# Attention queries: rotary rows crossed by four DMAs instead of two matrix products, and attended values in two portions in half of the pairs

## What is computed

```python
q = rms_norm(hidden_states @ wq_a, q_a_norm_w) @ wq_b      # rank 64, then 16 heads of 64 + 64
q_nope, q_pe = (q[..., :QK_NOPE], q[..., QK_NOPE:])
...
def rotate_half(x):
    x1, x2 = jnp.split(x, 2, axis=-1)
    return jnp.concatenate([-x2, x1], axis=-1)

def apply_rope(x, cos, sin):
    b, h, s, d = x.shape
    x = x.reshape(b, h, s, d // 2, 2).transpose(0, 1, 2, 4, 3).reshape(b, h, s, d)
    return x * cos + rotate_half(x) * sin
...
attn = jnp.einsum('bhqd,bhkd->bhqk', query_states, key_states) * SOFTMAX_SCALE
attn = jax.nn.softmax(attn.astype(jnp.float32), axis=-1)
out = jnp.einsum('bhqk,bhkd->bhqd', attn, value_states)
```

## Time and profile before

| | us |
|---|---|
| three runs, median (lowest to highest) | 1085.58 (1083.63 to 1086.48) |
| the profiled execution | 1089.22 |
| its span | 1087.4 |
| busy in the span: PE, DVE, ACT, POOL | 1014.7, 739.5, 518.5, 477.3 |

### The profile page before, as it was taken

One profiled execution on the slowest core, in us unless ns is written; L12 is line 12 of the kernel. 1 busy time (PEld: TensorE's weight loads), 2 busy tenths in 40 slices (PEclk: granted clock), 3 DMA queues, 4 the chain that ended last, 5 costly groups with the idle time before them and its releaser, 6 DMA issues.

```text
span 1087.4 us, 22864 instructions
## 1 busy us (share of the span) xinstructions
PE 1014.7 (93%) x6183; PEld 802.6 (74%) x6184; DVE 739.5 (68%) x1677; ACT 518.5 (48%) x1133; POOL 477.3 (44%) x418
## 2 busy tenths in 40 slices
PE   5459999999889999999999999999999889999995
PEld 4438888887557777777778777777688558888884
DVE  7446666745577788877887788888556746766642
ACT  2033334422366677767776677777401214443421
POOL 3733444433343744646464644443125514443422
PEclk9989999999899999999999999999999999999998
DMA  9646454422101123222232313232576434545230
GB/s 332 171 156 152 106 112 112 105 49 30 59 1 49 41 78 99 79 69 73 76 99 79 85 54 98 80 98 79 178 235 216 177 112 112 159 109 112 47 57 8
DMA packets 88899, 112.57 MB, mean 104 GB/s; under 512 B 10257, under 2 KB 65809, under 8 KB 88785
## 3 DMA queue, kind: packets, MB, share of 16 engines
q1 hardware_dynamic: 73936, 94.20, 28.6%
q0 software_dynamic: 14304, 16.87, 9.0%
q10 hardware_dynamic: 576, 0.53, 0.2%
HBM read 64.14 MB, written 51.34 MB: 106 GB/s over the span
## 4 chain that ended last, share of the span: by engine, by line
PE 84%; DVE 8%; issue 3%; ACT 1%; DMA 1%; another core or an unknown queue 1%; POOL 1%; POOLq 0%; DVEq 0%; SPq 0%; ACTq 0%
PE bank L1766 11%; PE bank L1793 11%; PE bank L1583 7%; PE bank L1581 7%; PE bank L1585 7%; PE bank L1754 5%; PE bank L1756 5%; PE bank L1755 5%; PE bank L1593 4%; PE bank L1595 3%; PE bank L1594 3%; PE bank L1566 3%; PE bank L1866 3%; PE bank L1741 2%; PE bank L1742 2%
## 5 line engine op out<-in xcount | busy, mean ns | idle before, releaser
L929 ACT ACTIVATE shared<-bank,small 128x512 f32<-128x512 f32 x256 | 176.7, 690 | 90.8 <-DVE small L1394 89.8
L1394 DVE TENSOR_REDUCE small<-bank 128x1 f32<-128x512 f32 x256 | 174.9, 686 | 41.8 <-PE bank L1756 41.7
L846 ACT CAST split_rows_and_inner<-bank 128x512 fp32r<-128x512 f32 x78 | 45.8, 587 | 238.3 <-PE bank L1566 177.7
L1766 PE MATMUL bank<-constants,shared 128*128 128x128 f32 x1024 | 156.3, 275 | 2.3 <-ACT shared L929 0.7
L1766 PEld LDWEIGHTS bank<-constants,shared 128*128 128x128 f32 x1024 | 122.2, 141 | 45.0 <-issue 13.9
L1583 PE MATMUL bank<-expert_weights_low,split_rows_and_inner 128*128 x312 | 144.2, 462 | 0.0
L1585 PE MATMUL bank<-expert_weights_high,split_rows_and_inner 128*128 x312 | 143.1, 459 | 0.0
L1581 PE MATMUL bank<-expert_weights_high,split_rows_and_inner 128*128 x312 | 125.1, 401 | 2.7 <-DVE split_rows_and_inner L1173 2.5
L1754 PE MATMUL bank<-expert_weights_high,shared_split 128*128 128x512 f32 x256 | 122.7, 479 | 2.4 <-POOL shared_split L672 1.4
L663 POOL TENSOR_TENSOR shared<-shared 128x512 f32<-128x512 f32 x32 | 41.3, 1289 | 189.0 <-DVE shared L1404 185.5
L1178 DVE TENSOR_TENSOR split_rows_and_inner<-bank,split_rows_and_inner 128x512 fp32r<-128x512 f32 x78 | 53.9, 692 | 100.9 <-ACT split_rows_and_inner L846 98.9
(11 more groups left out here) (201 smaller groups left out, 2194.5 us busy)
## 6 DMA issues: line engine op xcount, KB each, us to landing
rows_by_expert<-empty_rows SPq DMA_DIRECT2D x34, 516.0 KB, 5.3
expert_weights<-w SPq DMA_DIRECT2D x32, 512.0 KB
shared<-rows_by_expert SPq DMA_DIRECT2D x78, 129.0 KB
expert_weights<-wo SPq DMA_DIRECT2D x16, 512.0 KB
shared<-inverse_sums SPq DMA_DIRECT2D x64, 128.0 KB, 2.9
attended_transposed<-shared SPq DMA_DIRECT2D x32, 256.0 KB, 5.1
expert_weights<-attended_transposed SPq DMA_DIRECT2D x2, 2048.0 KB, 10.8
shared<-attended_transposed SPq DMA_DIRECT2D x2, 2048.0 KB
```

The costliest lines, as they stand in the source:

```text
L929: nc.scalar.activation(prob[k % 4], bank[k % 4][:, :], ACT.Exp, bias=negmax[:, k % 8:k % 8 + 1], accum_out=psum[par][:, hh * GT + qt:hh * ...
L1394: V.tensor_reduce(negmax[:, k % 8:k % 8 + 1], bank[k % 4][:, :], AX.X, ALU.max, negate=True).then_inc(max_ready, 1)
L1766: last = tr(bank[4 + k % 2][:, c * P:(c + 1) * P], prob[k % 4][:, c * P:(c + 1) * P], ident)
```

## The change

1. The products of part 1 are left out for pairs 2 to 31. In their place ACT copies part 0 from bank 7 to SBUF (`queries_unturned`, at k = 4, in pair 0 at k = 5, behind the preparation's copy and ahead of the exponential). SP moves it with four DMAs of 32 partitions each, which cross the halves, into the buffer ropeB (`turn_queries`), and DVE multiplies that by sine. The sign is in the table of sines now. The second rope product of DVE goes from k = 7 to k = 0 of the next pair. DVE's first rope product waits for ACT's copy of the same bank.
2. On SP `spread` is cut into `inverse_out` and `inverse_back`, and the four DMAs with their waits stand between them.
3. POOL makes the high and low part of two of three weights from pair 2 on; four one-time DVE instructions that write the turned weights write two pairs' and not eight pairs' worth.
4. In pairs p > 0 with remainder 0, 3, 4 or 7 by eight and in the last eight (`apart`), the attended values are made in two portions of 16 matmuls, one at k = 1 and one at k = 4 behind the scores. There `take_output` moves from k = 2 to k = 6, and DVE's copy of tile 4 stands behind the row maximum and not ahead of it. Waits for the buffers of tiles 0 to 3 now look at the first portion (`o_half`).

```diff
     c[:, C_COS:C_SIN] = np.tile(cos.T, (4, 1))
-    c[:, C_SIN:C_ALL] = np.tile(sin.T, (4, 1))
+    c[:, C_SIN:C_ALL] = np.concatenate([-sin.T, sin.T, -sin.T, sin.T])
     ids = (np.arange(NT)[None, :] * P + np.arange(P)[:, None]).astype(np.int32)
...
             return bank[(7, 6, 3)[part]] if among(p, 0) else bank[7]
+
+        def apart(p):
+
+            return p > 0 and (p // PAIRS + 1 == B or p % PAIRS in (0, 3, 4, 7))
...
-            def spread(p, par):
+            def turn_queries(p):
+
+                sp.wait_ge(unturned_sb, p - 1)
+                sp.wait_ge(rope_ready, p)
+                for a in range(4):
+                    b = a + 1 - 2 * (a % 2)
+                    sp.dma_start(ropeB[a * HALF:(a + 1) * HALF], unturned[b * HALF:(b + 1) * HALF]).then_inc(turned_in, 16)
+
+            def inverse_out(p):
                 sp.wait_ge(invT_sb, p + 1)
                 sp.dma_start(invd[p:p + 1, :].rearrange("a (k q) -> (a k) q", k=8), invT).then_inc(inv_stored, 16)
+
+            def inverse_back(p, par):
                 sp.wait_ge(inv_stored, (p + 1) * 16)
...
                 load_prep(g)
-            spread(0, 0)
-            spread(1, 1)
+            for p in range(2):
+                turn_queries(p + 2)
+                if p == 1:
+                    inverse_back(0, 0)
+                inverse_out(p)
+            turn_queries(4)
+            inverse_back(1, 1)
             load_prep(3)
                 store(p, p % 2)
-                spread(p + 2, p % 2)
+                inverse_out(p + 2)
+                if p + 5 < NPAIR:
+                    turn_queries(p + 5)
+                inverse_back(p + 2, p % 2)
                 empty_rows(p)
...
                 store(p, p % 2)
-                spread(p + 2, p % 2)
+                inverse_out(p + 2)
+                inverse_back(p + 2, p % 2)
             sp.wait_ge(o_psum, NPAIR)
...
-                src = wpair[:, p % PAIRS, :, :]
+                parts_ = slice(0, 3) if among(p, 0, 1) else slice(0, 3, 2)
+                src = wpair[:, p % PAIRS, parts_, :]
                 if p > 1:
                     pool.wait_ge(qz_psum, p - 1)
-                nc.gpsimd.tensor_copy(wch[par], src).then_inc(wc_high, 1)
+                nc.gpsimd.tensor_copy(wch[par][:, parts_, :], src).then_inc(wc_high, 1)
                 pool.wait_ge(wc_high, p + 1)
                 pool.sem_inc(pool_issue, 1)
-                nc.gpsimd.tensor_tensor(wcl[par], src, wch[par].bitcast(F32), ALU.subtract).then_inc(wcur_ready, 1)
+                nc.gpsimd.tensor_tensor(wcl[par][:, parts_, :], src, wch[par][:, parts_, :].bitcast(F32),
+                                        ALU.subtract).then_inc(wcur_ready, 1)
...
                 if k == 2 and not among(p, 0):
-                    act.wait_ge(o_psum, p)
+                    act.wait_ge(o_half, p)
                 nc.scalar.copy(pT[:, pT_place(par, k), :, :],
...
                 nc.scalar.copy(qh[par][hh][rows_], query_bank(p, 2)[rows_, :]).then_inc(qz_high, 1)
+
+            def queries_unturned(p):
+                act.wait_ge(qa_psum, p + 1)
+                if not among(p, 2):
+                    act.wait_ge(turned_in, (p - 2) * 64)
+                nc.scalar.copy(unturned, bank[7][:, :]).then_inc(unturned_sb, 1)
...
                             high_keys(b, 2, 6)
+                    if k == (5 if first else 4) and p + 2 < NPAIR:
+                        queries_unturned(p + 2)
                     if not (last and k > 5):
...
                                     norm_w[:, 0:1], None, ALU.mult)
-                    last = V.tensor_scalar(wpair[:, :, 1, at + (1 - two) * HALF:at + (2 - two) * HALF], src[:, :, hh, :],
-                                           norm_w[:, 0:1], -1.0 if two else 1.0, ALU.mult, ALU.mult)
+                    last = V.tensor_scalar(wpair[:, 0:2, 1, at + (1 - two) * HALF:at + (2 - two) * HALF], src[:, 0:2, hh, :],
+                                           norm_w[:, 0:1], None, ALU.mult)
             last.then_inc(wa_ready, 1)
...
                         dve.wait_ge(rope_ready, p)
+                    if not among(p, 0, 1):
+                        dve.wait_ge(unturned_sb, p - 1)
                     V.tensor_tensor(ropeA, query_bank(p, 0)[:, :], qcos, ALU.mult).then_inc(ropeA_sb, 1)
                 else:
-                    dve.wait_ge(qb_psum, p + 1)
-                    V.tensor_tensor(ropeB, query_bank(p, 1)[:, :], qsin, ALU.mult).then_inc(ropeB_sb, 1)
+                    if among(p, 0, 1):
+                        dve.wait_ge(qb_psum, p + 1)
+                        turned = query_bank(p, 1)[:, :]
+                    else:
+                        dve.wait_ge(turned_in, (p - 1) * 64)
+                        turned = ropeB
+                    V.tensor_tensor(ropeB, turned, qsin, ALU.mult).then_inc(ropeB_sb, 1)
...
                 if k == 0 and not among(p, 0, 1):
-                    dve.wait_ge(o_psum, p - 1)
+                    dve.wait_ge(o_half, p - 1)
                 if k == 4 and not among(p, 0):
...
                         ropes(1, k - 1)
+                    if k == (6 if apart(p) else 2) and not first:
+                        take_output(p - 1, 1 - par)
                     if k == 2 and not first:
-                        take_output(p - 1, 1 - par)
                         invert_sums(p - 1, 1 - par)
                         ropes(p + 2, 0)
-                    if k == 7 and not among(p, NPAIR - 2, NPAIR - 1):
-                        ropes(p + 2, 1)
-                    if k in BY_DVE:
+                    if k == 0 and not first and not last:
+                        ropes(p + 1, 1)
+                    late_copy = k == 4 and apart(p)
+                    if k in BY_DVE and not late_copy:
                         copy_pT(p, par, k)
...
                         row_max(p * 8 + k + AHEAD, k + AHEAD)
+                    if late_copy:
+                        copy_pT(p, par, k)
                     if p // PAIRS + 1 < B:
...
                         pe.wait_ge(invT_sb, p - 2)
+                elif among(p, 1):
+                    pe.wait_ge((ropeA_sb, ropeB_sb)[part - 1], p + 1)
                 elif not among(p, 0):
-                    pe.wait_ge((ropeA_sb, ropeB_sb)[part - 1], p + 1)
+                    pe.wait_ge(ropeA_sb, p + 1)
                 to = query_bank(p, part)
...
-            def attend(p, par):
-
-                pe.wait_ge(v_kept, p // PAIRS + 1)
-                pe.wait_ge(raw_sb, p)
-                bank_back(p // PAIRS + 1, p % PAIRS, 1)
+            def attend(p, par, halves):
+
+                if 0 in halves:
+                    pe.wait_ge(v_kept, p // PAIRS + 1)
+                    pe.wait_ge(raw_sb, p)
+                    bank_back(p // PAIRS + 1, p % PAIRS, 1)
                 wait_pT(pe, p, BY_ACT[-1])
                 wait_pT(pe, p, BY_DVE[-1])
-                for half in range(2):
+                for half in halves:
                     for c in range(GT):
...
                                       values[:, p // PAIRS, c, :], pT[:, a:b + 1:b - a, c, :], start=(c == 0), stop=(c == GT - 1))
-                last.then_inc(o_psum, 1)
+                    last.then_inc((o_half, o_psum)[half], 1)
...
                     if k == 1 and not first:
-                        attend(p - 1, 1 - par)
+                        attend(p - 1, 1 - par, (0,) if apart(p) else (0, 1))
+                    if k == 4 and apart(p):
+                        attend(p - 1, 1 - par, (1,))
                     if k == 2 and not first:
...
                         queries(p + 2, par, 0)
-                    if k == 3 and b < B:
+                    if k == 3 and b < B and not apart(p) and not first:
                         pe.wait_ge(raw_sb, p)
...
                             turn_keys(b, 2, 6)
-                    if k == 6 and p + 2 < NPAIR:
-                        queries(p + 2, par, 1)
                     if k == 6 and j in (1, 2, 5):
...
             inverse_transpose(NPAIR - 1, 1)
-            attend(NPAIR - 1, 1)
+            attend(NPAIR - 1, 1, (0, 1))
```

4 lines of the change are left out of this document (added).

## The result

| | before | after |
|---|---|---|
| median, us (lowest to highest, runs) | 1086.2 (1080.45 to 1089.63, 20) | 1089.7 (1086.09 to 1093.63, 20) |
| ratio of the times, with its 95% interval | | 1.0036 [1.0023, 1.0049] |
| span of the profiled execution | 1087.4 | 1090.7 |
| from the first attended values to the last, us | 457.97 | 462.14 |

The change makes the kernel slower by 3.9 us (2.5 to 5.3): small, but outside zero. I had forecast 1085.4 us, no difference. The last line of the table counts from the first start of an attended group to the last, and takes in the 31 pairs; there the loss is 4.17 us, so it lies in the attention. What lies outside took 629.4 us before and 628.6 after.

What follows compares the result with a forecast made beforehand. PE's program was taken as the bound (84% of the span). Terms -8.3 + 2.9 - 3.0 + 8.2 summed to -0.2 us, so 1085.4 us from a median of 1085.58; range 1074 to 1093.

Steps and rivals of the forecast that it cites:

- The laden pairs, +8.2: 12 pairs with whole attended values: DVE waits for ACT's copy, +8.2 us; T is the start of tile 4's transposes.
- That is 0.15 us for a portion more: On PE, splitting the attended values into two portions costs 0.15 us a pair, 19 pairs, +2.9 us.
- it just holds, with 0.2 us in hand: Pairs with two portions: DVE's copy of tile 4, behind the second portion, still comes in time for PE's tile 6.
- rival 3: Pairs with two portions exceed the 0.2 us; PE waits at tile 6 and next pair's start, +5.7, 1091 us; chance 0.10.
- The stalls, -3.0: Portions take away PE's stalls in pairs of remainder 3 (0.67 us each) and 7 (0.51 us each), -3.0 us.
- The products, -8.3: Two query matmuls leave PE's path, 0.46 us a pair, counted for 18 pairs, -8.3 us.
- The DMAs, 0: Four crossing DMAs on SP land before DVE's second rope product needs them, 1.3 us in hand in plain pairs; cost 0.
- rival 1: DVE and ACT make up the 1.4 us wait in laden pairs: 1071.7 us, half swallowed 1078.5; chance 0.30.
- Rival 2: Crossing DMAs land late, 5.1 us instead of 2.9, and DVE's second rope product waits: +18, 1103 us; chance 0.10.
- Rival 4: DVE's second rope product and POOL keep each other out at a shared SBUF port: about +4, 1089 us; chance 0.07.

Runs made afterwards that it cites:

- laden_products: Changed kernel, but queries made in laden pairs get their turned rows by the two products as before, without crossing DMAs; 1081.12 us, ratio 0.9928.
- portions_only: Kernel before plus the two portions alone; all products stay, no crossing by DMA; 1089.06 us, ratio 1.0028.
- rope_late_laden_act: act_first with DVE's first rope product moved to the end of step 5 in pairs without two portions; 1080.43 us, ratio 0.9937 to the kernel before.
- dmas_behind: Changed kernel with the four crossing DMAs issued behind the return of the inverse sums in SP's queue; 1090.46 us, ratio 1.0031 to the kernel before.
- act_first: Changed kernel with ACT's new copy of the queries ahead of the preparation's copy in laden pairs; 1083.67 us, ratio 0.9955 to the kernel before.

## Why the prediction was wrong

The sum was -0.2 us and the kernel lost 3.9. Its terms, one by one:

- **The laden pairs, +8.2: right, in size and in every place.** By remainder 1, 2, 5, 6 the table gives +0.48, +0.01, +1.26, +0.97 where I had +0.5, 0, +1.3, +0.9; over the 12 pairs the lengths add up to +8.3. In pair 13, T is 513.76 and the first rope product starts at 515.17, T + 1.41 (I had 1.35), the copy of tile 4 at T + 2.0 (2.0), tile 6 at T + 2.84 (2.83), the lower half of the keys at T + 4.41 (4.4). laden_products confirms the whole by undoing it. These rows are from DVE's timeline of after:

```profile
515.17 0.69 DVE L1440 TENSOR_TENSOR shared<-bank,constants 128x512 f32<-128x512 f32 x1 [1.42 <-ACT expert_weights L979]
515.78 0.68 DVE L1470 COPY shared<-bank 128x512 f32<-128x512 f32 x1
...
518.17 0.68 DVE L1376 TENSOR_TENSOR expert_weights_low<-bank,expert_weights_high 128x512 fp32r<-128x512 f32 x1
```

- **"That is 0.15 us for a portion more": the step that failed.** It is 0.29 to 0.30. The working took the gap ahead of the group and the dearer transposes behind it, and held the 32 matmuls to cost the same in two halves. They cost 0.15 more (3.76 against 3.61), and portions_only, where the products and the old path of the queries stay, gives 0.29 in all. In 17 pairs that is 17 x 0.15 = 2.6 us of the miss. In the last two, pairs 30 and 31, the second portion hardly costs: they take 13.31 and 10.88 us where they took 13.13 and 10.95, 0.1 us for both.
- **The margin at the copy of tile 4, "it just holds, with 0.2 us in hand": held there, and missed one step on.** Tile 6 is not late (713.31 - 712.12 = 1.19, as forecast). But the two copies and the maximum behind them are, by way of the exponential and ACT's copy of tile 6, and the next pair's first transposes start 0.31 behind the last score matmul and not 0.23: +0.09 by the timelines, in 17 pairs 1.5 us. The products that are gone had hidden this: in portions_only, with the same portions, these transposes start 0.23 behind. That is the second half of rival 3's mechanism, at a third of its price. The last score matmul and these transposes in PE's timeline of after:

```profile
715.33 0.40 PE L1806 MATMUL bank<-expert_weights_high,shared_split 128*128 128x512 f32 x1
715.64 0.63 PE L1816 MATMUL bank<-constants,shared 128*128 128x128 f32 x4
```

- **The stalls, -3.0:** remainders 3 and 7 are down to 14.25, the length of every plain pair, so this is right. In remainder 0 I left the small stall as it was, but it is 14.78, where 14.72 - 0.46 + 0.30 + 0.09 = 14.65 would be, 0.13 us in each of two pairs. It is also another stall. Before, the next pair's first tile started 0.54 behind the last score matmul; now PE waits for the inverted sums at k = 2, as in rope_late_laden_act, and this start in pair 16 comes 0.62 behind the score matmul:

```profile
556.77 0.27 PE L1850 MATMUL bank<-constants,small 128*8 128x128 f32 x1 [0.22 <-DVE small L1475]
```

- **The products, -8.3:** 66 in place of 96. That a pair of products is worth 0.46 where no other engine ends last is read off plain pairs: 14.33 - 0.46 + 0.30 + 0.09 = 14.26, measured 14.25.
- **The DMAs, 0: right.** I took 2.9 us for the landing and 2.2 for the issue; after has 2.0 and 2.47 (below). The sentence from the Trainium skill ("DMA: Bandwidth & Descriptors", "Anatomy of one DMA") gave an estimate of 2.2 us for the landing, nearer than my row was; that section's fit is for DMAs issued by GpSimd, and these are SP's. dmas_behind adds 0.6 us and more to it in plain pairs without loss. The margin is not endless: with the landing of 3.8 us in act_first one pair came out 0.6 us longer. The issues of DMAs of after (KB each, us to landing), then SP's queue in pair 13:

```profile
shared<-inverse_sums SPq DMA_DIRECT2D x64, 128.0 KB, 3.0
...
shared<-expert_weights SPq DMA_DIRECT2D x120, 64.0 KB, 2.0
```

```profile
515.07 2.47 SPq L535 DMA_DIRECT2D shared<-expert_weights  x4
517.58 1.23 SPq L544 DMA_DIRECT2D shared<-inverse_sums  x2
```

With the corrections the sum is -8.3 + 17 x 0.30 + 0.1 + 17 x 0.09 - 3.0 + 8.2 + 2 x 0.13 = +3.9 us, against 3.9 in the times. The 4.17 us of the attention leave out pair 0, whose products' 0.46 lie ahead of the first attended values: +4.4 by the sum. The price of a portion alone, or the 0.09 alone, would have left the sum below the 3.3 us that I called no difference; it took both.

The rivals: rival 1 (DVE swallows the wait) fell with the laden pairs, which are longer by all that was forecast. Rival 2 fell with the landing of 2.0 us. Rival 4 asked for a loss at L1448, whose mean is 680 ns; but POOL is idle during every one of them, so the case in which both work at once never came up, and no run here shows what it costs. Rival 3 is the one that holds in part: no wait at tile 6, and less of one at the next pair's start than I gave it. I gave 0.10 to it and 0.24 to slower as a whole; the doubt about a portion's price, which I had as one number without a range, is what that was short of.

What stays open: why 16 matmuls take more than half of the time of 32; the 3.6 us by which the times of laden_products fall below what its attention saves; and whether the late first rope product would pay together with the two portions in plain pairs, which no run has.

## What to carry to other kernels

A group of matmuls that is split pays at both ends of each part and inside: price the split from the two group lengths, or give its price a range, since it is multiplied by the number of groups. When an instruction gets a new wait, count what is queued behind it on its engine, and move it behind that queue if whoever reads its result needs it only later; here that one move turned 14.6 us of loss into 12.7 us of gain. And look at what an edit sets free: the move was closed by bank 7 before the products were gone, and open after.

## What the runs showed of the hardware

One more portion of 16 matmuls (128 x 64 weights, 256 columns) costs PE 0.15 us inside and 0.15 us around it, at a granted clock of 1.00. The second attended group alone takes 1.88 us where half of the whole would be 1.80.

Four DMAs of 64 KB each within SBUF land 2.0 us after their issue (1.9 to 3.0), sooner than the 2.9 to 3.0 us of 128 KB out of DRAM, and each holds SP's queue for 0.62 us.

The same instructions outside the stretch from the first attended values to the last took 629.4 us in the profile of before and 622.9 in that of portions_only (1082.2 - 459.34), which doesn't touch them, and part of it is the clock ahead of the attention. From 280 to 300 us the granted clock was 0.75 in the first row (before) and 0.83 in the second (portions_only):

```profile
280.00:300.00 20.00, 15.60 (x77) 11.83 (x77) 12.68 (x37) 7.58 (x13) 8.08 (x10) 0.75 0.09 29
```

```profile
280.00:300.00 20.00, 16.19 (x79) 10.85 (x80) 13.99 (x35) 10.24 (x16) 8.37 (x9) 0.83 0.08 27
```

A single span of this kernel can so be off by 6 us, while the lengths of the same pair in the first two batches agree to 0.05 us (but for pair 7 of act_first, with its late DMA); for edits of the attention the lengths are the better measure.
